# Look-ups of an embedding kernel, one slice a batch, with a chunk moved into the tile before

## The reference, cut to what matters

```python
e = jnp.stack([tbl_0[ids[:, 0]], ..., tbl_38[ids[:, 38]]], axis=1)   # 2048 x 39 x 32
p = e[:, ROW, :]; q = e[:, COL, :]                    # the 741 pairs i < j
z = jnp.einsum('bpc,apc,bpa->bp', p, w, q)            # w: 32 x 741 x 32
h = jnp.concatenate([z, dense_ctx], axis=1)           # 757 wide
h = jnp.maximum(h @ W_top1 + b_top1, 0.0)             # 512
h = jnp.maximum(h @ W_top2 + b_top2, 0.0)             # 256
y = h @ W_top3
```

## Time and profile before

| what | value |
|---|---|
| median of 3 runs | 841.4 us (837.88 to 843.4) |
| profiled execution, its time | 841.64 us |
| its span | 839.4 us |
| PE busy | 729.7 us, 87% |
| DVE busy | 634.9 us, 76% |
| POOL busy | 426.0 us, 51% |
| ACT busy | 94.4 us, 11% |
| chain that ended last | PE 59%, DVE 20%, DMA 10%, issue 7% |

### The profile page before, as it was taken

The page is one execution under the profiler, slowest core; times in us unless marked ns, Lnnn a source line. Parts: engine busy times, 40 slices in busy tenths (PEclk is TensorE's granted clock), DMA queues, the critical chain, the costliest instruction groups (busy, mean ns, idle before and its releaser), DMA issues.

```text
span 839.4 us, 11277 instructions
## 1 busy us (share of the span) xinstructions
PE 729.7 (87%) x4378; PEld 286.2 (34%) x4378; DVE 634.9 (76%) x792; ACT 94.4 (11%) x170; POOL 426.0 (51%) x463
## 2 busy tenths in 40 slices
...
PEclk9686859799999999999999999999999999999999
...
GB/s 194 163 232 298 64 243 85 314 273 296 281 154 259 263 170 134 159 161 190 159 168 243 183 170 132 161 159 188 158 261 218 201 158 134 156 135 116 109 0 1
DMA packets 75353, 149.88 MB, mean 179 GB/s; under 512 B 13261, under 2 KB 22560, under 8 KB 75172
## 3 DMA queue, kind: packets, MB, share of 16 engines
...
HBM read 115.49 MB, written 33.62 MB: 178 GB/s over the span
## 4 chain that ended last, share of the span: by engine, by line
PE 59%; DVE 20%; DMA 10%; issue 7%; ACT 2%; ACTq 2%; SPq 0%; DVEq 0%
PE z_ps L548 19%; PE u_ps L524 18%; DVE prod L821 11%; DVE one_hot L809 7%; PE m_ps L561 7%; PE t_ps L503 6%; DMA e<-scratch 4%; DMA w_rows<-h 3%; PE m_ps L563 2%; DMA zT<-in_tbl_dram 2%; PE t_ps L484 2%; DMA scratch<-parts 1%; PE u_ps L583 1%; DVE parts L775 1%; PE u_ps L592 1%
## 5 line engine op out<-in xcount | busy, mean ns | idle before, releaser
L821 DVE TENSOR_TENSOR prod<-u_ps,eT 128x1024 f32<-128x1024 f32 x400 | 469.4, 1216 | 126.8 <-PE u_ps L524 125.9
L371 POOL DMA_INDIRECT e_rows<-in_tbl_dram,idx x384 | 383.4, 998 | 299.2 <-DVE prod L821 224.3
L524 PE MATMUL u_ps<-e,w 128*128 128x512 f32 x800 | 260.8, 437 | 70.9 <-DVE prod L821 34.4
L548 PE MATMUL z_ps<-prod,sel 128*32 128x512 f32 x1600 | 263.4, 613 | 0.0
L524 PEld LDWEIGHTS u_ps<-e,w 128*128 128x128 f32 x800 | 133.1, 191 | 230.4 <-DVE prod L821 120.9
L503 PE MATMUL t_ps<-one_hot,tb 125*32 125x512 bf16 x1560 | 140.9, 409 | 25.2 <-DVE one_hot L809 25.0
L809 DVE TENSOR_SCALAR one_hot<-hot_idx,row 125x512 bf16<-125x512 f16 (+2 forms) x320 | 133.1, 475 | 7.5 <-PE t_ps L503 4.5
L503 PEld LDWEIGHTS t_ps<-one_hot,tb 125*32 125x32 bf16 x1560 | 53.4, 100 | 107.8 <-issue 55.5
L548 PEld LDWEIGHTS z_ps<-prod,sel 128*32 128x32 f32 x1600 | 43.5, 109 | 136.4 <-issue 124.5
L561 PE MATMUL m_ps<-zT,w1s 128*128 128x512 f32 x144 | 75.5, 625 | 0.8 <-ACT h L703 0.8
L642 ACT CAST parts<-t_ps 128x512 fp32r<-128x512 f32 (+1 forms) x40 | 23.5, 587 | 282.6 <-PE t_ps L503 206.5
...
## 6 DMA issues: line engine op xcount, KB each, us to landing
...
```

Source lines behind the costliest of these rows:

```text
L371: pool.indirect_dma_start(e_rows[:, r, n, D * q:D * q + D], None, tables[f], bass.IndirectOffsetOnAxis(ap=idx[:, t, f * TPG + n:f * TPG + ...
L524: last = nc.tensor.matmul(u_ps[:, s % 2, place, :], w4[:, p % WR, (u % PW) * P:(u % PW + 1) * P], e4[:, E4_SLOT[g], j - C * g, :], start=T ...
L548: last = nc.tensor.matmul(z_ps[D * quad:D * quad + D, z % 2, :], sel[:, D - 1 - row:2 * D - 1 - row], prod[:, (NS * t + n) % PR, place, :] ...
L821: nc.vector.tensor_tensor(prod[:, s % PR, :, :], u_ps[:, s % 2, :, :], e, ALU.mult).then_inc(s_mul, 1)
```

## The change

The kernel computes the same. Five edits:

1. `OTHER_TILES` takes one slice a batch where it took two, through most of the tile. Chunk 7 is looked up in the tile before (batches 37 to 45 of it), as chunks 1 and 2 already were, and for that `eT` has a fifth second place (`TWO_PLACES`). Chunk 1 for the next tile is taken in batches 20 to 27, chunk 2 in 29 to 35, chunk 8 in 1 to 9. Chunk 0 for the next tile is turned in batch 46 (it was 42), chunk 3 for the next tile in batch 48 (it was batch 0 of its own tile; in tile 1 it still is). In tile 0 slices stay in twos; tile 0 now takes 48 slices (it took 38), the last tile 10 (it took 20).
2. The pieces of the layers fall by the same rule into other batches: one each, in batches 3 to 8, 10 to 25, 28, 30 to 34, 36 to 40 and 47; in the last tile in 3 to 8, 10 to 35, 37 and 38. Before, batches 11, 12, 13, 15 and 16 had two.
3. The layers' weights are loaded in batch 44 of tile 0; `pause` lies in their place, and SP waits for the last pause.
4. A table is loaded as 112 + 13 partitions, by two transfers for each field. Tables 2 and 7 are loaded by SP, 1 and 8 by ACT.
5. The opening of DVE and ACT: the one-hots of chunk 1 no longer stand behind the first step on table 7, and ACT takes chunk 1 ahead of table 7.

```diff
-XE = 4
+TWO_PLACES = (0, 1, 2, 3, 7)
...
-FIRST_TILE = ((7, 0, None, (0, 0, 0, 1, 1, 1, 2, 2, 2, 2)), (3, 0, 3, ()), (8, 0, None, (5, 5, 6, 6, 7, 7, 8, 8, 9, 9)),
-              (4, 0, 14, ()), (5, 0, 21, ()), (6, 0, 28, ()), (9, 0, 35, ()),
-              (1, 1, None, (36, 37, 38, 38, 39, 39, 40, 40, 41, 41)), (0, 1, 42, ()), (2, 1, 43, (43, 44, 45, 45, 46, 46, 47, 47)))
-OTHER_TILES = ((3, 0, 0, ()), (7, 0, None, (1, 1, 2, 2, 3, 3, 4, 4, 5, 5)), (8, 0, None, (6, 6, 7, 7, 8, 8, 9, 9, 10, 10)),
-               (4, 0, 14, ()), (5, 0, 20, ()), (6, 0, 27, ()), (9, 0, 35, ()),
-               (1, 1, None, (36, 37, 38, 38, 39, 39, 40, 40, 41, 41)), (0, 1, 42, ()), (2, 1, 43, (43, 44, 45, 45, 46, 46, 47, 47)))
+FIRST_TILE = ((7, 0, None, (0, 0, 0, 1, 1, 1, 2, 2, 2, 2)), (3, 0, 3, ()), (8, 0, None, (4, 4, 5, 5, 6, 6, 7, 7, 8, 8)),
+              (4, 0, 13, ()), (1, 1, None, (14, 14, 15, 15, 16, 16, 17, 17, 18, 18)), (5, 0, 20, ()), (6, 0, 28, ()),
+              (2, 1, 29, (29, 29, 30, 30, 31, 31, 32, 32)), (9, 0, 36, ()),
+              (7, 1, None, (37, 37, 38, 38, 39, 39, 40, 40, 41, 41)), (0, 1, 46, ()))
+SECOND_TILE = ((3, 0, 0, ()),)
+OTHER_TILES = ((8, 0, None, (1, 2, 3, 4, 5, 6, 7, 8, 9, 9)), (4, 0, 12, ()), (5, 0, 19, ()),
+               (1, 1, None, (20, 21, 22, 23, 24, 25, 26, 26, 27, 27)), (6, 0, 28, ()),
+               (2, 1, 29, (29, 30, 31, 32, 33, 34, 35, 35)), (9, 0, 36, ()),
+               (7, 1, None, (37, 38, 39, 40, 41, 42, 43, 44, 45, 45)), (0, 1, 46, ()), (3, 1, 48, ()))
...
+MLP_WEIGHTS_BATCH = 44
+TABLE_SPLIT = ((0, 112), (112, HP))
...
-                    if t == 0 and b == 12:
+                    if t == 0 and b == MLP_WEIGHTS_BATCH:
+                        sp.wait_ge(s_pause, PAUSES)
...
+                    for a, b in TABLE_SPLIT:
+                        act.dma_start(room[a:b, at:at + n * D], rows[a:b, :]).then_inc(s_table[HOT_CHUNKS.index(g)], 16)
...
             weights_high(1)
+            take_chunk((0, 1))
             table_high(7)
             weights_rest(1)
             table_middle(7)
-            take_chunk((0, 1))
             take_chunk((0, 0))
...
             for k in range(OS):
                 one_hot_slice((0, 1), k)
+            table_rest(2)
+            for k in range(OS, slices_of(1)):
+                one_hot_slice((0, 1), k)
             table_low(2)
             weights_low(1)
-            table_rest(7)
-            for k in range(OS, slices_of(1)):
-                one_hot_slice((0, 1), k)
-            table_low(7)
             split_chunk((0, 1))
             for k in range(OS):
                 one_hot_slice((0, 2), k)
+            table_rest(7)
+            table_low(7)
             split_chunk((0, 0))
```

More of the change, by code:

```diff
@@ L133 @@
 BEGIN = (1, 0, 2)
-FIRST_TILE = ((7, 0, None, (0, 0, 0, 1, 1, 1, 2, 2, 2, 2)), (3, 0, 3, ()), (8, 0, None, (5, 5, 6, 6, 7, 7, 8, 8, 9, 9)),
-              (4, 0, 14, ()), (5, 0, 21, ()), (6, 0, 28, ()), (9, 0, 35, ()),
-              (1, 1, None, (36, 37, 38, 38, 39, 39, 40, 40, 41, 41)), (0, 1, 42, ()), (2, 1, 43, (43, 44, 45, 45, 46, 46, 47, 47)))
-OTHER_TILES = ((3, 0, 0, ()), (7, 0, None, (1, 1, 2, 2, 3, 3, 4, 4, 5, 5)), (8, 0, None, (6, 6, 7, 7, 8, 8, 9, 9, 10, 10)),
-               (4, 0, 14, ()), (5, 0, 20, ()), (6, 0, 27, ()), (9, 0, 35, ()),
-               (1, 1, None, (36, 37, 38, 38, 39, 39, 40, 40, 41, 41)), (0, 1, 42, ()), (2, 1, 43, (43, 44, 45, 45, 46, 46, 47, 47)))
+FIRST_TILE = ((7, 0, None, (0, 0, 0, 1, 1, 1, 2, 2, 2, 2)), (3, 0, 3, ()), (8, 0, None, (4, 4, 5, 5, 6, 6, 7, 7, 8, 8)),
[3 rows of a table added]
+SECOND_TILE = ((3, 0, 0, ()),)
+OTHER_TILES = ((8, 0, None, (1, 2, 3, 4, 5, 6, 7, 8, 9, 9)), (4, 0, 12, ()), (5, 0, 19, ()),
[3 rows of a table added]
 LAST_TABLE_BATCH = 1
+MLP_WEIGHTS_BATCH = 44
+TABLE_SPLIT = ((0, 112), (112, HP))
 def chunks_of_tile(t):
-    return [x for x in (OTHER_TILES if t else FIRST_TILE) if t + x[1] < NT]
+    lists = (FIRST_TILE, SECOND_TILE + OTHER_TILES) + (OTHER_TILES,) * (NT - 2)
+    return [x for x in lists[t] if t + x[1] < NT]
 ORDER = [(0, g) for g in BEGIN] + [(t + nxt, g) for t in range(NT) for g, nxt, turn, slices in chunks_of_tile(t)]
@@ L154 @@
 assert len(ORDER) == NT * NG == len(POS)
+PAUSES = PACED_FROM - 1 - sum(TPG * len(gathered(c)) for c in GATHERED[:2])
 def rows_count(c):
@@ L275, in tower @@
         y_sb = h1[0:1, 0, :]
+        pause = w1s[:, 0, :]
         zroom = zT[:, 1, :, :].rearrange("p k n -> p (k n)")
@@ L347, in e_slot @@
         def e_slot(t, g):
-            return NG + g if t % 2 and g < XE else g
+            return NG + TWO_PLACES.index(g) if t % 2 and g in TWO_PLACES else g
         def step_after(t, g):
@@ L394, in bring_piece, with load_table @@
                              ).then_inc(s_w4[n % WR], 16)
+            def load_table(g):
+                room = table_room(g)
+                for x, (q, n) in enumerate(HOT_TABLES[g]):
+                    at = (HOT_ROWS[g, x] - HOT_ROWS[g, 0]) * D
+                    rows = tables[C * g + q].rearrange("(p k) c -> p (k c)", k=n)
+                    for a, b in TABLE_SPLIT:
+                        sp.dma_start(room[a:b, at:at + n * D], rows[a:b, :]).then_inc(s_table[HOT_CHUNKS.index(g)], 16)
             def load_hot_indices(c):
@@ L430, in _ @@
             sp.dma_start(row8[:, :], hot_rows).then_inc(s_row8, 16)
+            load_table(2)
             sp.wait_ge(s_id16, 1)
@@ L438, in _ @@
             load_hot_indices((0, 2))
+            load_table(7)
             bring_piece(0, 0)
@@ L642, in take_chunk @@
                 nc.scalar.copy(parts[0:rows, n % 2, 0, :], t_ps[0:rows, :]).then_inc(s_eh, 1)
-                before = t - 2 if g < XE else t - 1
+                before = t - 2 if g in TWO_PLACES else t - 1
                 if before >= 0:
```

11 lines of the change are left out of this document (2 added, 9 removed).

## The result

847.7 us (median of 18 runs) against 841.5 (18 runs of the kernel before): ratio 1.0066, 95% interval 1.0049 to 1.0082. Forecast were 816, a range of 800 to 832, and faster with 0.90. The profiled execution took 845.0 (span 842.9) where that of before took 841.6: +3.4 instead of -25.4.

A forecast was written before the change was run, and what follows sets the result against it. DVE was taken to bound the look-up batches, PE those with pieces, the rest being waits for stacked chunks. -13.7 - 16.9 + 13.3 + 6.5 - 2.5 + 0.9 - 11 - 2 = -25.4 from 841.4 gave 816, range 800 to 832.

The forecast's parts named there:

- opening: Before the first multiplication: chunk 1's look-ups no longer wait for table 7, most gain lost on ACT; -2, between +3 and -8.
- the new wait: Starts of tiles 1 to 3: PE waits for chunk 0, stacked late; 4.0 each for tiles 2 and 3, 5.3 after tile 0, +13.3.
- tile 0 without its end: Tile 0 before its last batches: +6.5 for added slices, -2.5 and +0.9 around chunk 3's wait, -11 at chunk 8.
- Pricing by the batch: All tiles: a batch costs the larger of its PE and DVE times; slice and piece 3.60, tiles 1 and 2 sum to 172.7.
- slice and piece do not fit: Rival, 0.08: in batches with both, coupling through `u_ps` makes each cost 4.1, not 3.6; 840, no change.
- There remain 0.9, too short to drop the clock.: Batch 13, tiles 1 to 3: chunk 8's path of 10.2 against batches 10 to 12 at 9.3 leaves 0.9, clock kept.
- down by 11: Tile 0, wait for chunk 8: complete a batch sooner, without the layers' weights beside it; 0.6 of wait remains, -11.
- the fourth rival: Chance 0.12: DMA still binds tile 0, chunk 8's data or chunk 1's indices come late; 8 of the 11 stay, 824.
- the term of +6.5: Tile 0, batches 14 to 49: ten more slices 7.4, one more split 0.6, next tile's first look-ups -1.5.
- Little of the 8 is left: Opening: chunk 1 taken near 36 rather than 44.24, but ACT's queue order leaves chunk 2 near 54 instead of 55.14.
- the third rival: Chance 0.11: tables' 125 partitions load few DMA engines and hold up the rest; opening -8 instead of -2, 810.
- the bound of +19: Upper bound for the wait at three tile starts: the 6.4 of chunk 8 in tile 0 at each.

The follow-up runs named there:

- four-mends kernel: Changed kernel with next tile's chunk 0 turned in batch 37, stacking one batch sooner, chunk 8 complete in batch 8, tile 0's slices one a batch: 800.6 us, 0.951.
- the kernel with sooner stacking: Changed kernel with every chunk's stacking issued one batch after it is complete instead of two: 835.3 us, 0.992 of the kernel before.

## Where the prediction failed, by its own steps

The differences add up to what was missed (us; boundary and batch-13 losses are against the same batches of the four-mends kernel):

| step | forecast | measured |
|---|---|---|
| opening | -2 | -16.0 |
| the new wait, three tile starts | +13.3 | 7.2 + 8.8 + 7.0 = +23.0 |
| what remains at batch 13, three tiles | +2.7 | 4.4 + 5.8 + 4.6 = +14.7 |
| tiles 1 and 2 without these, each | 172.7 | 173.7, 173.1 |
| tile 3 without these | 159.5 | 162.4 |
| tile 0 without its end | -6.1 | +10.7 |

The errors: -14.0 + 9.7 + 12.0 + 1.4 + 2.9 + 16.8 = 28.8, which takes -25.4 to +3.4. That the total came out near no change is luck: the opening gained 14.0 more than forecast and hid a third of the 42.8 that the other terms lost; with the old opening the same lists stand at 1.023.

- **Pricing by the batch held.** A slice with a piece costs 3.65, PE full, and 172.7 stands against 173.7 and 173.1; with the waits gone whole tiles take 174.0 and 173.6. The count behind it was off by one: seven batches have a slice alone and four have neither, which with the turn in batch 29 hardly moves the sum. The 2.9 of tile 3 lie in batches 0 to 2 (10.5 against 9.6), 3 to 8 (22.8 against 21.6, mostly batch 5 at 4.5) and those with one piece (88.1 against 87.2). The rival "slice and piece do not fit" is refuted.
- **"The new wait"** is the step that failed first: "Its path is chunk 8's: 10.2". The mechanism was there, its place too; the path is 12.6 to 13.1. What stands around it on SP's queue is part of the reason: the store takes 4.1 between a piece and an index load, 3.6 or 3.7 beside one of them, and 2.1 beside neither. I had put 0.4 on the index load and nothing on the piece.
- **"There remain 0.9, too short to drop the clock."** The same number failed again: 12.0, 13.4 and 12.4 in tiles 1 to 3 instead of 10.2. By moving chunk 8 from an even to an odd batch, the change let the piece in front; with the piece put back behind, the path was 11.1 and 10.3 in tiles 2 and 3, but still 12.1 in tile 1, so this is shown for two tiles of three. PE's idle time crossed from 1.54 (clock kept, in the kernel with sooner stacking) to 2.47 and more (halved): 0.9 became 4.4 to 5.8. Had I read the order on SP's queue around chunk 8, part of this would have been seen.
- **Tile 0** has the largest error. Its batches 0 to 5 cost 3.9 more instead of 1.6 less: the opening alone, with the old lists, already makes 1.9 and, in its repetition, 4.0 of this, as the wait for chunk 3 does not move all the way with the start. The wait for chunk 8 shrank as forecast, from 6.41 to 0.78. Yet batches 8 to 13 went only from 26.9 to 22.0, not down by 11, because in batch 13 DVE waits for the index rows of chunk 1 and then builds its first two slices:
```profile
139.15 0.49 PE L549 MATMUL u_ps<-e,w 128*128 128x512 f32 x1 [0.78 <-DMA e<-scratch]
...
143.19 3.17 DVE L833 TENSOR_SCALAR one_hot<-hot_idx,row 125x512 bf16<-125x512 f16 x6 [2.28 <-DMA hot_idx<-hot]
```
  The wait of 2.28 is what the fourth rival named ("the indices of chunk 1", 0.12), at under a third of its price of 8; the other traces with these lists show 1.5 to 2.4. The 3.1 us of one-hots belong to the term of +6.5: with them and the 11.9 more of batches 14 to 48 it measured 15.0. A slice of chunk 1 costs DVE 1.3 to 1.6 there (2.61 to 3.17 for two) and not the 0.92 taken from chunk 8; at batch 20 ACT stood 8.9 us in front of a load of weights that waits for a written block, and in batch 21 PE stood 3.0, as the rows of chunk 5 waited for ACT.
- **The opening.** "Little of the 8 is left" was wrong: chunk 1 was taken 16 sooner and chunk 2 9.7. And the third rival (slow whole transfers), given 0.11 and -8 for the whole opening, was borne out: the split is worth 6.9 by itself and 9.3 on top of order and queues. The row was there: two write issues of 5.47 us where others take 1.2. A DMA share of 0.97 over 19 us was read as "nearly all were busy", but from 65 to 69 us it is 0.72 and 0.73.
- The range was too narrow: one path length, taken from one tile, carried both the new wait and what remains at batch 13, and the bound of +19 for the new wait was left out of the range. Both erred to the same side, by 9.7 and 12.0.

What stays open: what the standstill is; what sets the wait for chunk 3 in tile 0; why the path of chunk 8 stayed long in tile 1 with the new order; and why two slices of chunk 1 in tile 0 cost DVE 2.61 to 3.17 where one slice costs 1.00.
